# Expert loop of a fused fusion layer on Trainium2: blocks 2 and 3 of a group through one 1024-column gelu into SBUF, VectorE multiplying block 2 from there

## The reference

```python
z = jnp.einsum('nd,sdr->nsr', xf, P)
scores = jnp.einsum('nsr,smr->nsm', z, C)
topv, topi = jax.lax.top_k(scores, K)
w = jax.nn.softmax(topv, axis=-1)
h = jax.nn.gelu(jnp.einsum('nsr,nskrh->nskh', z, W1g) + b1g)
yl = jnp.einsum('nskh,nskhr->nskr', h, W2g) + b2g
comb = jnp.einsum('nskr,nsk->nsr', yl, w)
out = jax.nn.gelu(comb @ G1 + g1b) @ G2 + g2b
```

## Time and profile before

| what | value |
|---|---|
| median of 3 executions | 971.04 us (970.57 to 973.81) |
| the profiled execution | 974.09 us |
| its span | 972.3 us |
| TensorE matmuls busy | 899.8 us, 93% of the span |
| VectorE busy | 671.3 us, 69% |
| ScalarE busy | 593.7 us, 61% |
| GpSimd busy | 477.6 us, 49% |
| mean granted TensorE clock | 0.963 of full speed |

### The profile page before, as it was taken

How to read it: one execution, slowest core, us unless ns; L and a number is a source line. 1 busy time by engine, 2 the same in 40 slices (tenths; PEclk the granted TensorE clock), 3 DMA queues, 4 the chain that set the end, 5 groups by cost and what they waited for, 6 DMA issues and landing times.

```text
span 972.3 us, 16073 instructions
## 1 busy us (share of the span) xinstructions
PE 899.8 (93%) x5394; PEld 417.3 (43%) x5394; DVE 671.3 (69%) x1670; ACT 593.7 (61%) x870; POOL 477.6 (49%) x446
## 2 busy tenths in 40 slices
PE   3599999999999978799999999999999999999997
PEld 1267777777777756222222322322232223222322
DVE  4346555666666667677777888787777877876764
ACT  0221211125332245688888889898889888987774
POOL 0133434233335525477755666556556655664442
PEclk8699999999999977799999999999999999999999
DMA  9300001000000176766778787879788878888672
GB/s 269 118 1 1 1 2 69 2 1 1 1 1 15 30 129 97 227 204 213 220 221 248 229 243 239 249 226 247 213 250 232 254 208 243 235 246 276 231 235 97
DMA packets 87212, 151.32 MB, mean 156 GB/s; under 512 B 30083, under 2 KB 54276, under 8 KB 86481
## 3 DMA queue, kind: packets, MB, share of 16 engines
q1 hardware_dynamic: 86158, 147.04, 50.8%
q10 hardware_dynamic: 972, 3.24, 2.6%
HBM read 135.99 MB, written 14.25 MB: 155 GB/s over the span
## 4 chain that ended last, share of the span: by engine, by line
PE 78%; ACT 10%; DVE 5%; issue 2%; DMA 1%; SPq 1%; POOL 1%; ACTq 0%; DVEq 0%; POOLq 0%
PE ps L760 17%; PE ps L699 14%; PE ps L737 8%; PE ps L422 8%; PE ps L430 5%; PE ps L489 4%; PE ps L481 3%; PE ps L498 3%; PE ps L539 2%; PE ps L459 2%; ACT ring L1057 2%; PE ps L511 2%; ACT L939 2%; DVE ring L1494 1%; ACT ring L1064 1%
## 5 line engine op out<-in xcount | busy, mean ns | idle before, releaser
L1696 POOL TENSOR_TENSOR ring<-ring,wbc 128x512 f32<-128x512 f32 x192 | 244.7, 1279 | 170.4 <-ACT ring L1064 162.4
L1494 DVE TENSOR_TENSOR ring<-ps,ring 128x1024 f32<-128x1024 f32 x192 | 235.0, 1224 | 109.4 <-PE ps L737 80.1
L699 PE MATMUL ps<-zst,w1st 99*128 99x512 bf16 x768 | 216.0, 388 | 18.0 <-ACT ring L1057 14.2
L760 PE MATMUL ps<-ring,w2cur 128*32 128x512 f32 x1536 | 205.6, 608 | 0.0
L1057 ACT ACTIVATE ring<-ps 128x1024 f32<-128x1024 f32 x192 | 197.2, 1027 | 6.4 <-PE ps L699 6.1
L1551 POOL TENSOR_TENSOR t<-t 128x768 f32<-128x768 f32 x48 | 87.4, 1832 | 204.4 <-DVE t L1185 204.4
L1066 ACT ACTIVATE ps<-ps 128x512 f32<-128x512 f32 x192 | 113.9, 593 | 59.2 <-PE ps L699 59.2
L699 PEld LDWEIGHTS ps<-zst,w1st 99*128 99x128 bf16 x768 | 72.0, 98 | 156.5 <-ACT ring L1057 34.6
L1497 DVE TENSOR_TENSOR ring<-ps,wbc 128x512 f32<-128x512 f32 x192 | 130.5, 680 | 1.4 <-DMA wbc<-w_rows 1.4
L737 PE MATMUL ps<-wst,sel 96*128 96x512 bf16 x384 | 119.0, 392 | 6.3 <-DVE ring L1494 5.4
L1183 DVE TENSOR_TENSOR t<-ps,rope 128x768 f32<-128x768 f32 x48 | 45.7, 952 | 110.1 <-PE ps L430 73.9
(11 more groups left out here) (166 smaller groups left out, 1149.5 us busy)
## 6 DMA issues: line engine op xcount, KB each, us to landing
wbc<-w_rows SPq DMA_DIRECT2D x192, 512.0 KB, 5.2
w2cur<-in_w SPq DMA_DIRECT2D x48, 256.0 KB, 4.6
w_parts<-wp SPq DMA_DIRECT2D x72, 64.0 KB, 3.3
zst<-z_parts SPq DMA_DIRECT2D x72, 64.0 KB, 5.1
wst<-w_parts SPq DMA_DIRECT2D x72, 64.0 KB, 4.6
w1st<-w_parts ACTq DMA_DIRECT2D x12, 256.0 KB
z_parts<-zp SPq DMA_DIRECT2D x6, 384.0 KB, 5.2
out_h<-h SPq DMA_DIRECT2D x12, 192.0 KB, 4.5
```

Of the source, the lines that this page charges most:

```text
L699: return pe.matmul(bank(to), w1st[0:99, 4 * a + j, col:col + P], zst[0:99, (i // 2) % 2, j, :], start=True, stop=True)
L760: mm = pe.matmul(bank(YBANK, 0, 512, 32 * j, 32 * j + 32), w2cur[:, n, j, :], ring[:, (4 * g + j) % RING, :], start=False, stop=(n == 7 an ...
L1494: dve.tensor_tensor(v, ps[:, WBANK * 512:WBANK * 512 + 1024], v, ALU.mult).then_inc(s["duo_done"], 1)
L1696: pool.tensor_tensor(ring[:, slot, :], ring[:, slot, :], wbc[:, g % 4, 1, :], ALU.mult).then_inc(s["tri_done"], 1)
```

## The change

In the changed kernel the first-layer blocks 2 and 3 of a group lie in banks 2 and 3, and PBANK is bank 4. TensorE makes them together, behind the gates of blocks 0 and 1 (`pair_firsts`), after one wait for the gelu of the group before. ScalarE applies one gelu of 1024 columns to both and writes ring slots 2 and 3. VectorE multiplies block 2 in the ring, with both inputs in SBUF, and GpSimd block 3, as before; both wait for the same semaphore, `pair_gelu`. Ahead of the loop TensorE makes the four first blocks before the scores of tile 5, and ScalarE copies these scores after the gelus of group 0.

```diff
-JBANK, PBANK, TBANK, WBANK, YBANK = 2, 3, 4, 5, 7
+JBANK, TBANK, PBANK, WBANK, YBANK = 2, 3, 4, 5, 7
...
                 if m >= 2:
-                    sp.wait_ge(s["two_full"], 16 * (m - 1))
+                    sp.wait_ge(s["pair_full"], 16 * (m - 1))
...
-            def tri_first(g):
+            def pair_firsts(g):
 
                 if g > 0:
-                    pe.wait_ge(s["tri_gelu"], g)
-                else:
-                    pe.wait_ge(s["res"], PAIRS - 1)
-                first(g, 3).then_inc(s["tri_full"], 1)
-
-            def two_first(g):
-
-                if g > 0:
-                    pe.wait_ge(s["two_done"], g)
-                first(g, 2).then_inc(s["two_full"], 1)
+                    pe.wait_ge(s["pair_gelu"], g)
+                first(g, 2)
+                first(g, 3).then_inc(s["pair_full"], 1)
...
+            duo_firsts(0)
+            pair_firsts(0)
+            pe.wait_ge(s["res"], PAIRS - 1)
             scores(LEAD, PBANK)
-            duo_firsts(0)
             duo_gates(0)
-            tri_first(0)
-            two_first(0)
...
                 if g + 1 < GROUPS:
                     duo_firsts(g + 1)
-                    tri_first(g + 1)
                 if g >= 2 and g % 16 != 2:
                     second(g - 2)
...
                 if g + 1 < GROUPS:
                     duo_gates(g + 1)
-                    two_first(g + 1)
+                    pair_firsts(g + 1)
...
-            act.wait_ge(s["sel_cast"], 1)
-            copy_scores(LEAD, PBANK)
             for g in range(GROUPS):
...
-                act.wait_ge(s["tri_full"], g + 1)
-                act.activation(ring[:, slot + 3, :], bank(TBANK), ACT.Gelu_apprx_tanh).then_inc(s["tri_gelu"], 1)
-                act.wait_ge(s["two_full"], g + 1)
-                act.activation(bank(JBANK), bank(JBANK), ACT.Gelu_apprx_tanh).then_inc(s["two_gelu"], 1)
+                act.wait_ge(s["pair_full"], g + 1)
+                act.activation(ring[:, slot + 2:slot + 4, :].rearrange("p a n -> p (a n)"),
+                               ps[:, JBANK * 512:JBANK * 512 + 2 * BLK], ACT.Gelu_apprx_tanh).then_inc(s["pair_gelu"], 1)
+                if g == 0:
+                    copy_scores(LEAD, PBANK)
...
-                dve.wait_ge(s["two_gelu"], g + 1)
+                dve.wait_ge(s["pair_gelu"], g + 1)
                 dve.wait_ge(s[f"spread{g % 4}"], 16 * (g // 4 + 1))
-                dve.tensor_tensor(ring[:, slot + 2, :], bank(JBANK), wbc[:, g % 4, 0, :],
+                dve.tensor_tensor(ring[:, slot + 2, :], ring[:, slot + 2, :], wbc[:, g % 4, 0, :],
                                   ALU.mult).then_inc(s["two_done"], 1)
...
-                pool.wait_ge(s["tri_gelu"], g + 1)
+                pool.wait_ge(s["pair_gelu"], g + 1)
```

More of the change, by code:

```diff
@@ L185, in fused_layer @@
                  "t_top t_mr p_dist e_done n_done p_em p_w hi_done r_done mid_done lo_done sel_cast "
-                 "duo_full duo_gelu duo_w duo_done two_full two_gelu two_done tri_full tri_gelu tri_done "
+                 "duo_full duo_gelu duo_w duo_done pair_full pair_gelu two_done tri_done "
                  "second_done y_kept u_full u_done o_full "
```

## The result

The changed kernel takes 1011.83 us (median of 4, 1007.12 to 1012.76) against 971.04 before: 1.0404 times the time, with a 95% interval of 1.0366 to 1.0443 (the ratio goes by all executions; that of the two medians is 1.042). The forecast was 1012. The profiled execution took 1010.97 us with a span of 1008.6 (before 974.09 and 972.3, so +36.3 in the span), at the same mean granted clock (0.964, before 0.963).

A forecast was written before the change was run, and what follows sets the result against it. TensorE, busy 93%, was taken as the bound; port-contention stalls of 8.3 + 24 + 6 in the iterations, 1 in the plain ones and 1.3 in the tail gave +40.6, so 971 + 41 = 1012, 8 in 10 for 975 to 1040.

The forecast's parts named there:

- V: VectorE's multiply of block 2, 680 ns before; forecast to rise to 1100 or more in the mean.
- G: GpSimd's multiply of block 3; forecast to exclude VectorE's multiply of block 2 while either runs.
- Who goes first: VectorE's block 2 multiply wins in plain groups at no cost; GpSimd's wins after back-to-back gelus, making VectorE wait 1.15.
- The 0.13 let in early: A blocked operation enters some 0.13 before GpSimd's recorded end; the rival whole-instruction rule would give about 1018.
- What becomes late: VectorE's 1024-column multiply, which the next gates pair waits for; TensorE's idle there was to grow by tens of us.
- M: VectorE's 1024-column multiply, one input in SBUF; forecast to stay at 1224 ns but come late for the gates.
- T: ScalarE's gelu of block 3 in the kernel before; TensorE's wait on it was forecast to disappear.
- The walk: One iteration with tile work followed group by group: gates stalls 0.64, 0.76, 0.42, 0.08, 0.81; 25.5 against 22.76, +2.75.
- These two cancel within 1 us: Longer gelu at the exponentials, up to +8.5, against the saved block 3 gelu wait at the gates copy, -8.0.
- P: ScalarE's new 1024-column gelu of blocks 2 and 3; forecast to delay the exponentials by 0.45, 19 times.
- D: ScalarE's 1024-column gelu of blocks 0 and 1; after the exponentials forecast to come 0.45 or more later.
- The marks: Signs: block 2 multiply's mean 1100 ns or more, maximum near 1.9 us; iterations 4 to 18 taking 24 to 26.

The follow-up runs named there:

- e13_no_mul_no_v: Changed kernel with both GpSimd's multiply of block 3 and VectorE's multiply of block 2 left out; 978.6 us, ratio 1.0086.
- e6_t_behind_products: Kernel before with only block 3's first layer moved behind the products of group g-2; 966.2 us, ratio 0.9958.
- e2_ring_old_order: Kernel before with block 2's gelu writing the ring and VectorE multiplying it from there, orders and waits kept; 994.2 us, ratio 1.0240.
- e3_no_gpsimd_mul: Changed kernel with GpSimd's multiply of block 3 replaced by an empty instruction; 985.1 us, ratio 1.0151.
- e4_gpsimd_after_v: Changed kernel with GpSimd's multiply of block 3 waiting for VectorE's multiply of block 2 of the same group; 1008.7 us, ratio 1.0380.

## Why the prediction was right

- **The mechanism**: shown. V beside a reading G is held back, beside memsets or nothing it is not. The part of the loss that needs G is 26.7 us by medians, both multiplies together 33.2 (1011.8 - 978.6). The prediction put nearly all of its 40.6 there.
- **Who goes first**: right in both cases, V by 0.04 in the plain groups, G by 0.51 at 605.70.
- **The 0.13 let in early**: G of 605.70 ends at 606.97; less 0.13 and with V's 0.68 that makes 607.52, and V ended at 607.51 (606.21 + 1.30). The whole-instruction rule, counted to the recorded end, would give 607.65; the row was the better price. It holds for all 90 V over 760 ns in the kernel after: each ended 0.68 us after a moment 0.126 to 0.136 us ahead of the recorded end of the GpSimd operation.
- **What becomes late**: right. The matmuls' idle before gates, released by M, grew by 33 us (32 over 400 to 960 in both), and the wait on T is gone; plain groups stayed at 2.40.
- **The walk**: too high, and it missed an operation. It forecast +2.75 for iterations 7, 11 and 15, which are odd intervals, and took 2.0 for the others; the odd ones measured +1.9, the even +1.8, those with last layers +2.2. Of these 0.3, 0.2 and 0.7 are there without either multiply (e13_no_mul_no_v), so the meetings cost 1.5 to 1.6. The stall at the second gates pair was 1.24 and not 0.76: VectorE's copy L1326, which reads and writes SBUF in front of the next M, stands behind GpSimd's work too (0.49 for 0.18). The later terms, 0.42, 0.08 and 0.81, did not occur: an odd interval has no third stall. The walk missed that GpSimd's distances (L1575, 611.17 to 612.23, and L1577 after them) hold G back, so that V starts before it at 612.34.
- **"These two cancel within 1 us"**: the step that failed. P 0.45 longer at the exponentials was set against 0.42 saved at the gates copy. Without both multiplies 8.3 us remain, where the prediction had under 1, beside 1 for the plain groups. The cost of the longer P was sized well: TensorE stands 7.1 us longer for D, where up to 8.5 was forecast. The gain was too large: the saved wait by itself is worth 5.7 us by medians (971.85 - 966.17, e6_t_behind_products) and not 8.0. And the 3.4 us by which the gates wait longer for M even without the multiplies had no term at all. Neither P nor the order was tried alone.
- **The sum**: iterations 4 to 18 were put at 32.3. The fourteen intervals from the fifth exponentials measured 27.31, the four before them 7.14 (forecast 6), the rest 3.60 (forecast 2.3 and iteration 18; 1.66 of it is the clock in the last layers, for which the forecast has no term), the start -1.75 (forecast 0, bounds 1 each way; but the first exponentials of all the profiles lie between 405.3 and 412.3, so this term says nothing). 36.3 in the span against 40.6; that the medians differ by 40.8 is partly the profiled execution of before, 3.05 over its median. The overstated walk and the understated new order offset one another; that 1012 met 1011.83 so closely is luck.
- **The marks**: V's mean was to be 1100 or more and was 1009; its maximum, near 1.9, was 1.81. M is at 1216 ns. Intervals with the last layers take 27.5, over the 24 to 26 given, since they had 25.4 before.
- **The tail**: the last product is released by G, as forecast, with 1.20 of idle time, and comes 1.5 later after its last gates pair than before (forecast 1.3). The prediction says that V released it before, while the row names M; V ended last (961.45, M 960.86), so the prediction's reading stands. Timeline of the kernel after:

```profile
994.35 1.77 POOL L1687 TENSOR_TENSOR ring<-ring,wbc 128x512 f32<-128x512 f32 x1 [0.61 <-ACT ring L1054]
...
996.26 1.07 PE L753 MATMUL ps<-ring,w2cur 128*32 128x512 f32 x8 [1.20 <-POOL ring L1687]
```

**Open**: the 8.3 us of the new order, one edit at a time; the 6 us that memsets keep; the 9.2 us of the ring operand without G. A version that has the 1024-column gelu and a multiply of block 2 with one SBUF input would need block 2's bank free earlier, and was not tried.

## What to carry to other kernels

Before an operand is moved from PSUM to SBUF, look which engines read SBUF at that moment: here the same VectorE multiply, at 680 ns alone, cost the kernel 2.4% through its operand alone (e2_ring_old_order). Then ask who starts first in each kind of group: the same contention was free where VectorE was early and cost a stall of TensorE where it was late. ScalarE had 192 instructions fewer and 9.5 us less work here and nothing was gained, since it was not the bound; and the merged gelu ends 0.45 us later than the single one did, which the exponentials behind it felt.

## What the runs showed of the hardware

- A 128x32 VectorE copy in SBUF, 0.18 us alone, took 0.50 in the median in the changed kernel, 0.49 with G left out (e3_no_gpsimd_mul), so GpSimd's tile work is enough, and 0.83 with G after V (e4_gpsimd_after_v).
- A V that waited on a running GpSimd operation got the next turn. In all 90 stretched groups of the kernel after it was let in at the end of the GpSimd operation in progress, in 43 of them although another one started before V had ended: V at 606.21 got in although the cast of 606.91 followed G, and the cast took 0.86 (L1593, 0.39 at best). The same holds in 117 groups of e2_ring_old_order.
- Where both start within 0.02 us, the records do not tell who gets in: G did at 691.24 of e4_gpsimd_after_v, V at 614.67 of the kernel after, recorded 0.02 behind G.
- Two memsets of 1353 ns beside V leave its median at 692; a reading G of 1279 lifts its mean to 1009.
